# First maxima dealt out one per step beside the entropy model; the first projection with a program of its own

## The reference, cut to what matters

```python
def prelu(v, a): return jnp.where(v >= 0, v, a * v)
# layer 0: attention over the 4096 positions of each image
q = prelu(conv1x1(gn(x), w1, b1), a1)          # 24 rows
k = prelu(conv1x1(gn(x), w2, b2), a2)          # 24 rows
v = prelu(conv1x1(gn(x), wa, ba), aa)          # 192 rows
x = x + softmax(q.T @ k, axis=-1) @ v.T
# layer 1: entropy model, a small network of each channel's own (1-3-3-3-1)
def logits(t):
    for i in range(4):
        t = softplus(m[i]) @ t + b[i]
        if i < 3: t = t + tanh(f[i]) * tanh(t)
    return t
y = gn(x); lower, upper = logits(y - 0.5), logits(y + 0.5)
s = -sign(lower + upper)
x = x + maximum(abs(sigmoid(s * upper) - sigmoid(s * lower)), 1e-6)
```

## Time and profile before

| | before |
|---|---|
| median of 3 runs | 5024.87 us |
| the profiled execution | 5030.57 us |
| its span, from first to last instruction | 5028.8 us |
| busy: TensorE matmul, VectorE, ScalarE, GpSimd | 89%, 84%, 73%, 14% |
| mean granted clock of TensorE | 0.968 of full |
| image 0's setup, projection and first maxima | 0 to about 129 us |
| one pass of the loop | about 614 us |
| of it the 48 steps of the entropy model | about 184 us |

### The profile page before, as it was taken

One profiled execution on the slowest core, in us unless ns is written; L12 is line 12 of the kernel. 1 busy time (PEld: TensorE's weight loads), 2 busy tenths in 40 slices (PEclk: granted clock), 3 DMA queues, 4 the chain that ended last, 5 costly groups with the idle time before them and its releaser, 6 DMA issues.

```text
span 5028.8 us, 106046 instructions
## 1 busy us (share of the span) xinstructions
PE 4486.9 (89%) x38408; PEld 2990.4 (59%) x38408; DVE 4209.8 (84%) x5474; ACT 3649.6 (73%) x4008; POOL 693.8 (14%) x751
## 2 busy tenths in 40 slices
PE   4999879998899988999889997899978999799976
PEld 2788427873388733887247872588625886167831
DVE  4898789977999778997789978899688996889966
ACT  1667786768776687776876768766787767866788
POOL 5000300003000030101301012000220002101012
PEclk8999999998999999999899999999999999999988
DMA  2100440114310153001420115200242103410133
GB/s 50 39 20 20 98 101 19 33 32 103 88 30 22 35 114 76 28 28 37 112 75 23 31 43 117 62 26 28 55 116 50 33 20 72 107 46 29 33 80 97
DMA packets 154988, 280.18 MB, mean 56 GB/s; under 512 B 37441, under 2 KB 37825, under 8 KB 152706
## 3 DMA queue, kind: packets, MB, share of 16 engines
q1 hardware_dynamic: 154434, 272.94, 21.7%
HBM read 205.49 MB, written 50.33 MB: 51 GB/s over the span
## 4 chain that ended last, share of the span: by engine, by line
PE 55%; DVE 18%; issue 13%; ACT 9%; DMA 2%; SPq 2%; POOL 1%; DVEq 0%; ACTq 0%; POOLq 0%
PE ps L1293 10%; PE ps L1295 10%; PE ps L1297 10%; PE ps L1084 7%; PE ps L1245 6%; DVE mxp L990 5%; ACT th L654 4%; DVE th L929 3%; DVE arena L985 3%; ACT arena L647 3%; PE ps L1156 3%; PE ps L1170 3%; DVE mxp L975 2%; PE ps L1139 2%; DMA arena<-x2d 2%
## 5 line engine op out<-in xcount | busy, mean ns | idle before, releaser
L1293 PE MATMUL ps<-v_sb,arena 128*128 128x193 f16 x8192 | 2021.5, 247 | 11.4 <-DVE arena L985 11.4
L1295 PE MATMUL ps<-v_sb,arena 128*128 128x192 f16 x8192 | 2030.2, 248 | 0.0
L1297 PE MATMUL ps<-v_sb,arena 128*128 128x193 f16 x8192 | 2014.0, 246 | 0.0
L611 ACT ACTIVATE arena<-ps 128x1024 f16<-128x1024 f32 x1024 | 1049.8, 1025 | 932.9 <-PE ps L1084 932.7
L985 DVE TENSOR_TENSOR arena<-arena 128x1024 f16<-128x1024 f32 x1024 | 1294.2, 1264 | 244.0 <-ACT arena L614 243.7
L990 DVE TENSOR_REDUCE mxp<-ps 128x1 f32<-128x512 f32 x1792 | 1177.2, 686 | 50.3 <-PE ps L1245 40.3
L929 DVE SCALAR_TENSOR_TENSOR th<-th,gates,ps 128x1024 f32<-128x1024 f32 x768 | 950.8, 1275 | 226.5 <-ACT th L654 222.5
L614 ACT ACTIVATE arena<-ps 128x1024 f32<-128x1024 f32 x1024 | 1046.8, 1022 | 0.0
L1295 PEld LDWEIGHTS ps<-v_sb,arena 128*128 128x128 f16 x8192 | 796.1, 97 | 262.0
L654 ACT ACTIVATE th<-ps,biases 128x1024 f32<-128x1024 f32 x768 | 825.4, 1113 | 165.4 <-PE ps L1156 119.6
L1293 PEld LDWEIGHTS ps<-v_sb,arena 128*128 128x128 f16 x8192 | 793.4, 97 | 143.6 <-issue 19.3
(11 more groups left out here) (118 smaller groups left out, 3219.8 us busy)
## 6 DMA issues: line engine op xcount, KB each, us to landing
x<-x2d SPq DMA_DIRECT2D x1152, 64.0 KB, 2.4
arena<-x2d SPq DMA_DIRECT2D x768, 64.0 KB, 2.6
xp<-x_dram SPq DMA_DIRECT2D x18, 1536.0 KB, 13.3
shared<-x_dram SPq DMA_DIRECT2D x64, 384.0 KB, 3.8
x2d<-shared SPq DMA_DIRECT2D x64, 384.0 KB, 3.0
res<-x2d SPq DMA_DIRECT2D x96, 256.0 KB
out_dram<-res SPq DMA_DIRECT2D x96, 256.0 KB
kst<-shared SPq DMA_DIRECT2D x32, 256.0 KB, 5.1
```

The lines of the kernel that those rows point to most:

```text
L611: act.activation(e_hi[:, q % 4, :].rearrange("p (k n) -> p k n", k=2), sc, ACT.Exp)
L1293: pe.matmul(acc, eh, v_sb[:, m, 0:C + 1], start=(m == 0 and t % 2 == 0), stop=False, skip_group_check=True)
L1295: pe.matmul(acc[:, 0:C], eh, v_sb[:, m, VW:VW + C], start=False, stop=False, skip_group_check=True)
L1297: ins = pe.matmul(acc, el, v_sb[:, m, 0:C + 1], start=False, stop=(m == MT - 1), skip_group_check=True)
```

## The change

It has two parts.

**The loop.** The ten stack DMAs go out two per v, for v = 2 to 6. `negative`, `value` and GpSimd's `values` run one step later than `value_bank` (bank s+5 in step s). The maxima start in step 11 (FIRST_AT) and go one tile per step, s = 11 to 42: TensorE's matmul (`first_max`) stands between first_layer(s) and second_layer(s-1) and waits for the reduction of the tile two before; VectorE reduces that one tile at the end of its step. split_max is in step 43 (before 39), turn_max in 44 (before 41), rows_out in 45 (before 42).

**The start.** Three constants (`g6`, `w_raw`, `cols`) count on a semaphore of their own, `norm_in`, and are issued first; group norm 1 and TensorE wait for these alone. Softplus is cut in four pieces that VectorE runs between and behind the first maxima, ScalarE's part comes after its 24 banks, and GpSimd's coefficients wait for both. Image 0's maxima go in pairs through banks 2 to 7, pair g beside value bank 8+g for g = 0 to 7, the other eight pairs behind.

```diff
+NORM_DMAS, CONST_DMAS = 3, 6
-FIRST_AT = 22
-FIRST_GROUPS = MAXES // 2
+FIRST_AT = 11
@@ SP
+            for dst, src in ((g6_sb[:, :], g6), (w_raw[:, :, :], wall), (cols_sb[:, :], cols)):
+                sp.dma_start(dst, src).then_inc(norm_in, 16)
...
-                        if proj and 2 <= v < 2 + 2 * STACK_DMAS:
-                            stack((v - 2) // STACK_DMAS, (v - 2) % STACK_DMAS)
+                        if proj and 2 <= v < 2 + STACK_DMAS:
+                            for k in (2 * v - 4, 2 * v - 3):
+                                stack(k // STACK_DMAS, k % STACK_DMAS)
@@ ScalarE, image 0
+                    for n in range(BANKS):
+                        negative(n)
+                    act.wait_ge(set_step, 3)
+                    act.activation(sp_e, sp_abs, ACT.Exp, scale=-1.0).then_inc(set_act, 1)
+                    act.wait_ge(set_step, 4)
+                    act.activation(sp_l, sp_u, ACT.Ln).then_inc(set_act, 1)
+                    act.activation(gates[:, :, :], gates[:, :, :], ACT.Tanh).then_inc(set_act, 1)
@@ ScalarE, loop
-                    if proj and s + V_LEAD < VB:
-                        negative(QK + s + V_LEAD)
+                    if proj and s >= 1 and s - 1 + V_LEAD < VB:
+                        negative(QK + s - 1 + V_LEAD)
@@ VectorE, image 0
+                    for n in range(BANKS):
                         query(n)
+                        if n == BANKS - 2:
+                            next(weights)
+                        if n >= QK + VB // 2:
+                            reduce_two(n - QK - VB // 2)
+                    for g in range(VB // 2, MAXES // 2):
+                        reduce_two(g)
+                        if g == VB // 2 + 3:
+                            next(weights)
+                    split_max(0, 0)
+                    rows_out(0, 0, True)
+                    next(weights)
@@ VectorE, loop
+                        m = s - FIRST_AT
+                        if 0 <= m < MAXES:
+                            dve.wait_ge(max_mm, pj(BLOCKS * MAXES, m + 1))
+                            dve.tensor_reduce(mxp[...], ps[:, m % 2, :], AX_X, ALU.max).then_inc(max_red, 1)
+                        if m == MAXES:
                             split_max(pj(BLOCKS, 0), pj(BLOCKS * MAXES, 0))
+                        if m == MAXES + 2:
                             rows_out(pj(BLOCKS, 0), 0, l is None)
@@ TensorE
+                def first_max(m):
+                    if m == 0:
+                        pe.wait_ge(val_ready, pj(BANKS, BANKS))
+                    if m in (0, BLOCKS // 2):
+                        pe.wait_ge(stacks_in[m // (BLOCKS // 2)], ...)
+                    if m >= 2:
+                        pe.wait_ge(max_red, pj(BLOCKS * MAXES, m - 1))
+                    pe.matmul(ps[:, m % 2, :], qst[...], kst[...], start=True, stop=True).then_inc(max_mm, 1)
...
+                    for v in range(VB):
+                        value_bank(v)
+                        if v >= VB // 2:
+                            first_two(v - VB // 2)
+                    for g in range(VB // 2, MAXES // 2):
+                        first_two(g)
+                    turn_max(0, 0)
...
+                    if proj and 0 <= s - FIRST_AT < MAXES:
+                        first_max(s - FIRST_AT)
```

More of the change, by code:

```diff
@@ L581, in _ @@
         def _(act):
[L582 to L587, removed]
             def deviation1(b):
@@ L662, in phase_a @@
                         negative(n)
-                if l is not None:
-                    deviation2(l)
+                deviation2(l)
                 if proj:
-                    for n in range(3, 5 if l is not None else QK + V_LEAD):
+                    for n in range(3, 5):
                         negative(n)
[L668 to L673, removed]
+                act.wait_ge(gn2_step, l * GN2_STEPS + 16)
@@ L674, in phase_a @@
+                for i in range(LEAD):
+                    first_tanh(i)
                     if proj:
-                        for n in range(5 + LEAD, QK + V_LEAD):
-                            negative(n)
+                        negative(5 + i)
+                if proj:
+                    for n in range(5 + LEAD, QK + V_LEAD):
+                        negative(n)
                 for s in range(SLOTS + (1 if proj else 6)):
[L678 to L697, removed]
@@ L932, in phase_a @@
                 if l is None:
-                    for n in range(QK + V_LEAD):
+                    weights = softplus()
+                    for n in range(BANKS):
                         query(n)
[L935 to L957, removed]
+                        if n == BANKS - 2:
+                            next(weights)
+                        if n >= QK + VB // 2:
+                            reduce_two(n - QK - VB // 2)
@@ new lines, in phase_a @@
+                seen = dve.compute_val(l * 2 * BLOCKS + 2 * BLOCKS)
+                settle(dve)
+                dve.wait_ge(x2_stat, seen)
+                next(chain2)
+                if proj:
+                    query(1)
+                next(chain2)
+                if proj:
+                    query(2)
+                next(chain2)
+                next(chain2)
+                if proj:
+                    query(3)
+                next(chain2)
+                if proj:
+                    for n in range(4, QK + V_LEAD):
+                        query(n)
@@ new lines, in phase_a @@
+                    for g in range(VB // 2, MAXES // 2):
+                        first_two(g)
+                    turn_max(0, 0)
+                    pe.wait_ge(max_in, 16)
+                    scores(0, 0)
+                    scores(0, 1)
+                    return
+                pe.wait_ge(out_norm, l * BLOCKS + BLOCKS + START)
+                pe.wait_ge(x2_ready, l * 2 * BLOCKS + 2 * BLOCKS - 2 + START)
+                for h in range(2):
+                    turn_out(BLOCKS - 1, h)
+                if proj:
+                    qk_bank(0)
+                    qk_bank(1)
+                    qk_bank(2)
@@ new lines, in phase_a @@
+                averages2(l, 0)
+                if proj:
+                    qk_bank(3)
+                averages2(l, 1)
+                if proj:
+                    qk_bank(4)
+                pe.wait_ge(gn2_step, l * GN2_STEPS + 12)
+                for q in range(PER_H):
+                    ins = pe.matmul(ps[:, 6, 4 * q:4 * q + 4], sel_sb[:, q, :],
+                                    rsnm.rearrange("p h k -> p (h k)"), start=True, stop=True)
+                ins.then_inc(gn2_mm, 1)
+                if proj:
+                    for n in range(5, QK):
+                        qk_bank(n)
```

195 lines of the change are left out of this document (103 added, 92 removed).

## The result

| | before | after |
|---|---|---|
| median on the same chip, 4 runs each | 5028.20 us | 4973.27 us |
| span of the profiled execution | 5028.8 us | 4972.1 us |
| first layer of pass 0 | 542.75 us | 511.06 us |
| one pass, mean of the first six | 614.4 us | 610.7 us |
| its 48 steps, s = 0 to 47, mean of seven | 184.1 us | 180.4 us |

The ratio is 0.9891, with a 95% interval of 0.9874 to 0.9908: 55 us faster, where 98 were forecast. The start gave its 32 us. Each pass gave 3.7 instead of 9.4, and 7 x 5.7 = 40 us is nearly all of the 43 that are missing.

The account below looks back on a forecast made before the run. The chain of waits was taken as the bound, TensorE being more than half of the span. Start 32 us plus seven passes 66 made 98 off 5030.57, giving 4933; the forecast was 4930 us, range 4902 to 4970.

Parts of the forecast that it names:

- Step 1: Start: group norm 1 waits for three constants; with w_raw landing at 27.0 its chain starts at 27.3, gain 11.7 us.
- Step 2: Start: image 0's maxima beside the value banks, bank and pair 2.04 us, TensorE setting the pace; gain 23.6 us.
- Steps 3 and 4: Start: softplus behind rows_out loses 1.7 us; GpSimd's coefficients beside image 0's attention lose 1.5 us.
- Step 5: Pass, s = 11 to 29: VectorE stays under ScalarE, stretch falls to the control's 68.8 plus 1.2, gain 8.1 us.
- Step 7: Pass, s = 0 to 11: two stacks per v delay side loads, loss 3 us; later `negative` costs 0.
- Step 6: Pass, s = 29 to 43: VectorE bounds, stretch takes 47.6 us, gain 5.3.
- Step 8: End of a pass: split_max, turn_max and rows_out come later; loss 0.2 us for turn_max ahead of first_layer(45).
- The stacks take it back: Rival, 15%: side loads of v = 3 to 7 lose 8 us instead of 3, a pass gains 4.4; 4965 us.
- The clock: Rival, 5%: TensorE falls to half clock oftener in steps with maxima; slower, 5074 us with 14 such steps.
- The loop gives all: Rival, 12%: the stacks find slack and no side load is late; a pass gains 12.4 us, 4909 us.
- only the start is left: Rival, 3%: second layer behind first_max makes ScalarE wait, steps stay at 4 us; 4993 us.

Follow-up runs that it names:

- e6: The changed kernel with w_raw loaded in two DMAs (96 rows and one row), nothing else: 4972.7 us, ratio 0.9874.
- e7: The changed kernel with GpSimd's coefficients of the entropy model left out, two memsets in their place: 4969.4 us, ratio 0.9867.
- e2: The changed kernel with values, `negative` and `value` back in the step of their bank, maxima still from s = 11: 4949.7 us, ratio 0.9838.
- e4: The new start with the loop of the kernel before: 5004.1 us, ratio 0.9941.
- e12: The changed kernel with all ten stacks at v = 1 and nothing else, values still one step late: 4971.0 us, ratio 0.9883.
- e5: e2 with all ten stacks issued together at v = 1 instead of two each at v = 2 to 6: 4941.2 us, ratio 0.9814.
- e8: The changed kernel with e5's edits, w_raw in two DMAs and turn_max one step later: 4940.3 us, ratio 0.9816.
- e9: e5 with GpSimd's sums of a unit ahead of that step's values: 4925.6 us, ratio 0.9792.
- e11: e5 with 20 more small DMAs on SyncE's queue, four each at v = 2 to 6: 4941.9 us, ratio 0.9822.
- e10: e9 with w_raw in two DMAs: 4927.8 us, ratio 0.9796.

## Why the prediction was wrong, step by step

**Start.**
- *Step 1* held: chain at 26.0 (forecast 27.3), and e6 shows that w_raw set it, with 22.1 without. The Trainium skill (DMA: Bandwidth & Descriptors, "Why a DMA increments its semaphore by 16 and not by 1") gave the 97 rows one engine. e6 agrees: 96 rows and one row landed under the statistics.
- *Step 2*: maxima 36.9 us earlier, forecast 11.7 + 23.6 = 35.3. Bank and pair take 1.74, not 2.04: from the pair to the bank 0.43, from the bank to the next pair 1.31, where a bank alone had 1.42.
- *Steps 3 and 4* had the sum right and the parts wrong. Softplus costs 1.64 until the first subtraction, as forecast (1.7), and 1.0 more by the fifth, because ScalarE then waits 3.87 us for scores; GpSimd costs about 0.3, not 1.5.
The Trainium skill (SBUF — State Buffer, "Who interferes with whom") was a reason to fear this place. e7 puts it at 0.6 us over 128 subtractions here; GpSimd's coefficients ran from 98 to 157 us, beside the first of them only.
- Not in the forecast: the way from the last transposes of image 0 to the first layer of pass 0 takes 33.0 instead of 30.7 us. It begins at a lower clock (0.86 granted from 478 to 490 us, 1.00 at that place before), and the transposes take 1.85 instead of 1.07 us. What lowered it isn't shown, and it isn't the change's own: in the seven passes of the kernel before the same stretch takes 30.7 to 33.4.
- Sum: 36.9 - 1.6 - 1.0 - 0.3 - 2.3 = 31.7, forecast 32. That it meets the forecast so closely is luck: 1.6 us more from steps 1 and 2 stand against the 2.3 that weren't in it.

**Pass.**
- *Step 5* is the step that failed, by its term "On top 1.2: first_max(0) stands ahead of second_layer(10) and waits for the last value of step 10". The stretch s = 11 to 29 came to 74.8, 6.1 over the control of this run (68.7), not 1.2: 4.8 us a pass, 34 of the 43 that are missing. The mechanism is the one named; what was mis-sized is the wait, 5.5 us, with half clock behind it. I took the last value as done when its step is done, and took for granted that tile 0 needs it. It was last in ScalarE's list, behind an instruction that waited for GpSimd, and the delay of `value` by one step, also in the change, put it there. For the rest the step held: from 12 on 3.88 us a step, control 3.82, and VectorE under ScalarE.
- *Step 7* erred in place. Two stacks per v cost next to nothing in s = 0 to 11: e2 has 40.9 there with them, e4 40.7 with one per v. Of the 3 us forecast 0.2 came. The delay of values, which I priced at 0, costs 1.4 (42.3 against 40.9): it is the 1.71 us wait of value bank 13 shown above. The stacks' price is at s = 12 and was hidden in the changed kernel (e12).
- *Step 6*: 49.2 instead of 47.6, and 48.7 to 49.2 in all versions with the new loop. VectorE is full there, as forecast (48.3 us busy), but the count was short. Steps 29 to 33 take 14.7, since one more result (L911, 0.68) and a wait of 0.58 for ScalarE lie in them; 33 to 37 and 37 to 41 take 13.4 and 13.5. The last two steps, taken as half of four, have the logits of a whole unit and take 7.6, not 6.8.
- *Step 8*: 14.2 instead of 12.9 for 43-47, forecast 0.2 lost. It is 13.6 in three passes, as in e5 and e8, and 14.5 to 14.8 in the four in which the first layer of s = 45 runs at a low clock:

```profile
1293.60 0.22 PE L1105 MATMUL ps<-eye,mparts 128*12 128x128 f16 x1 [1.11 <-DVE mparts L869]
1293.79 1.89 PE L1200 MATMUL ps<-arena,w1s 64*64 64x512 f32 x8
```

For the 0.7 between 12.9 and 13.6 no run was made. VectorE's six instructions of split_max, 1.2 us, lie in this stretch now and lay in step 39 before; e8's wait for the gates behind them fits.

Three waits stood one behind the other at the same place of a pass: the last value, the stacks' bytes, GpSimd's list. With them taken away in this order (e2, e5, e9) the 48 steps fall from 180.4 to 176.7, 175.5 and 173.5, which is 26, 8 and 14 us for seven passes, and the ratio from 0.9891 to 0.9838, 0.9814 and 0.9792. Neighbouring intervals overlap, so the sizes of the last two are rough; their sum isn't. With all three away the loop gives 10.6 a pass (184.1 to 173.5), more than the 9.4 forecast, and the kernel takes 4925.6. The forecast was of a kernel without these waits. Stretch by stretch it isn't that kernel either: e9 has 40.9 in s = 0 to 11, where it has no stacks, 69.7 in 11 to 29 and 49.1 in 29 to 43, against 44, 70 and 47.6.

**Rivals.** *The stacks take it back* had the nearest time (4965) and the wrong reason. *The clock* didn't turn it: first layers at the low level stand at single steps (12 in every pass, 8, 24, 25 or 45 in some), never through a stretch, and the whole has 0.974. *The loop gives all*, 12.4 a pass, was reached by none. e4 rules out *only the start is left* (5004 against 4973).

## What to carry over

When a new matmul is put into a full list, its wait has to be followed through the lists of all engines, to the instruction that is last in the slowest of them; that the step is over is no bound. It has to be asked, too, whether the wait names only what the matmul needs. A wait that takes TensorE 5 us also hides what comes late under it: after it is removed, the next view to read is who waits now. Each of the three repairs here was one move in an engine's order. The second paid nothing without the first (e12); whether the third, GpSimd's order, would pay by itself wasn't run, and in the changed kernel it is part of the first wait's ring.

## What the hardware showed

- Side rows of four DMAs of 64 KB took 6.0 us from the last issue to the first layer with three DMAs of 256 KB just ahead of them, res and two stacks (e2), and 2.45 us with res and four DMAs of 4 KB there (e11), though the small ones held the queue longer than the stacks (3.02 against 1.73 us).
- A pair of maxima beside a value bank lengthened TensorE's rhythm by 0.32 us (1.74 against 1.42 a bank), though the pair itself holds it for 0.43: the bank behind it came 0.11 us sooner than a bank behind a bank.
- 3.3 to 4.6 us gained before pass 0 (e6, e8, e10, against the changed kernel, e5 and e9) didn't show in the time: the seven passes behind came out 3.9, 3.3 and 6.8 us longer in all. One execution of each was profiled, so this stays open.
